# A two-layer graph kernel: where the normalised rows of layer 0 are made and how they are turned

## The reference

```python
# layer 0, 4 heads of 64
h = relu(layernorm(x));  q, k, v = h @ Wq, h @ Wk, h @ Wv
attn = softmax(where(adj, q k^T / 8, -max));  x = x + (attn @ v) @ Wo + bo
# layer 1, 8 heads of 64
h = relu(layernorm(x));  m = h @ map_w.T + map_b;  n = m / |m| per head
cos_adj = (n n^T * ~adj > 0.1)
q, k = m @ q_w.T + q_b, m @ k_w.T + k_b;  p = softmax(where(adj, -1e10, q k^T / 8)) * keep
A = cos_adj * p;  s = h @ gcn_map_w.T + gcn_map_b
x = x + relu((A @ s) @ gcn_W.T / (A.sum(-1) + 1))
```

## Time and profile before

| | before |
|---|---|
| median of three runs | 3766.14 us (3765.32 to 3766.64) |
| the profiled execution | 3767.53 us, its span 3765.7 us |
| TensorE matmul busy | 3665.0 us, 97% of the span |
| VectorE, ScalarE, GpSimd busy | 72%, 45%, 36% |
| mean granted TensorE clock | 0.994 of full |
| queue of SyncE's DMAs | 380.73 MB, 30.4% of 16 engines |
| chain that ended last | PE 89%, DVE 5%, issue 4%, DMA 1% |

### The profile page before, as it was taken

The page is one execution under the profiler, slowest core; times in us unless marked ns, Lnnn a source line. Parts: engine busy times, 40 slices in busy tenths (PEclk is TensorE's granted clock), DMA queues, the critical chain, the costliest instruction groups (busy, mean ns, idle before and its releaser), DMA issues.

```text
span 3765.7 us, 101867 instructions
## 1 busy us (share of the span) xinstructions
PE 3665.0 (97%) x31020; PEld 3224.1 (86%) x31020; DVE 2723.6 (72%) x9432; ACT 1695.4 (45%) x5075; POOL 1357.2 (36%) x2069
## 2 busy tenths in 40 slices
PE   8999999999999999999999999999999999999997
PEld 5888888888888888888888888888888888888885
DVE  3777777777777777777777777777777777777765
ACT  2444444444444444444444444444444444444443
POOL 2333433433433333334334334334333333343331
PEclk9999999999999999999999999999999999999998
DMA  2223323233233233333232332322332333332323
GB/s 94 91 96 106 99 99 107 94 108 102 96 112 102 96 109 100 102 104 104 97 107 98 100 107 94 109 102 96 112 102 96 108 100 102 103 104 98 107 86 107
DMA packets 250601, 381.35 MB, mean 101 GB/s; under 512 B 41328, under 2 KB 173968, under 8 KB 250576
## 3 DMA queue, kind: packets, MB, share of 16 engines
q1 hardware_dynamic: 250304, 380.73, 30.4%
q0 software_dynamic: 272, 0.30, 0.0%
HBM read 179.61 MB, written 167.77 MB: 92 GB/s over the span
## 4 chain that ended last, share of the span: by engine, by line
PE 89%; DVE 5%; issue 4%; DMA 1%; DVEq 1%; POOL 0%; ACT 0%; SPq 0%; POOLq 0%; ACTq 0%
PE bank L949 35%; PE bank L957 19%; PE bank L973 14%; PE bank L981 8%; PE bank L942 7%; PE bank L1090 3%; DVE h L675 1%; DVE x_mid L824 1%; PE bank L1024 1%; PE bank L1102 1%; DVE rel L794 1%; PE bank L898 1%; PE bank L1096 1%; DVE mv L669 0%; DVE rec L785 0%
## 5 line engine op out<-in xcount | busy, mean ns | idle before, releaser
L605 ACT ACTIVATE att<-att,nmax 128x256 f32<-128x256 f32 x1024 | 508.1, 501 | 83.5 <-DVE nmax L760 83.5
L771 DVE SCALAR_TENSOR_TENSOR att<-bank,att 128x256 f32<-128x256 f32 x1024 | 404.9, 421 | 33.0 <-ACT att L605 18.3
L949 PE MATMUL bank<-gT,w_k 128*128 128x256 f32 x3072 | 417.2, 285 | 0.5 <-DVE k L841 0.5
L949 PE MATMUL bank<-gT,w_q 128*128 128x256 f32 x3072 | 414.6, 284 | 2.7 <-DVE w_k L698 1.4
L949 PEld LDWEIGHTS bank<-gT,w_map 128*128 128x128 f32 x3072 | 370.7, 188 | 34.3 <-issue 25.8
L949 PE MATMUL bank<-gT,w_map 128*128 128x256 f32 x3072 | 396.9, 285 | 1.1 <-DVE gT L801 1.1
L949 PE MATMUL bank<-hT,w_qkv 128*128 128x256 f32 x3072 | 392.6, 284 | 4.4 <-DVE hT L801 4.4
L949 PEld LDWEIGHTS bank<-gT,w_k 128*128 128x128 f32 x3072 | 386.7, 189 | 8.2 <-DVE k L841 0.7
L957 PE MATMUL bank<-w_v,gT 128*128 128x512 f32 x1536 | 385.2, 399 | 0.0
L949 PEld LDWEIGHTS bank<-hT,w_qkv 128*128 128x128 f32 x3072 | 373.2, 189 | 13.6 <-DVE w_o L689 4.8
L949 PEld LDWEIGHTS bank<-gT,w_q 128*128 128x128 f32 x3072 | 380.3, 189 | 3.7 <-DVE w_k L698 2.2
(11 more groups left out here) (136 smaller groups left out, 7042.9 us busy)
## 6 DMA issues: line engine op xcount, KB each, us to landing
scratch<-att SPq DMA_DIRECT2D x256, 512.0 KB, 2.6
uT<-scratch SPq DMA_DIRECT2D x1024, 128.0 KB, 3.0
x_in<-x SPq DMA_DIRECT2D x64, 512.0 KB, 3.7
x_res<-x_mid SPq DMA_DIRECT2D x64, 512.0 KB, 2.9
out<-x_res SPq DMA_DIRECT2D x64, 512.0 KB, 2.8
adj<-adj SPq DMA_DIRECT2D x64, 64.0 KB, 1.9
att<-gcn_map SPq DMA_DIRECT2D x1, 1024.0 KB, 10.9
att<-map_rows SPq DMA_DIRECT2D x1, 1024.0 KB, 6.4
```

Source lines behind the costliest of these rows:

```text
L605: s_.activation(e_sl, e_sl, ACT.Exp, bias=nmax1[:, p, c, e:e + 1], scale=-1.0, accum_out=esum1[:, p, c, e:e + 1]).then_inc(exp1_done, 1)
L771: v_.scalar_tensor_tensor(e_sl, in_blocks(gram_bank[e][:, c * N:c * N + N]), COS_THRESHOLD, e_sl, ALU.is_gt, ALU.mult, accum_out=usum1[:, ...
L949: last = t_.matmul(dst, w(ws, k)[:, t * 128:t * 128 + 128], rhs[:, rs, k, :], start=(k == 0 and i == 0), stop=(k == KT - 1 and i == 2))
```

## The change

The rows of layer 0 are no longer normalised by VectorE and turned by TensorE, except for the first graph. `norm0` moves to ScalarE, which computes relu(x * rstd - mean * rstd) straight into `h`, laid out in 32-column blocks. GpSimd makes the new operand `shift0` = -mean * rstd by two small operations behind `rstd0`. Two new VectorE steps, `hflip0` and `hflip1`, transpose `h` in 32x32 blocks in place; two new SyncE steps, `hsend` and `hfetch`, write `h` to DRAM (512 KB) and read it back in four DMAs, so that the blocks land in their places. `ht0a` and `ht0b` keep a place on ScalarE and VectorE only: they split the turned rows, now in SBUF, into high and low parts. The five tables are written anew around this.

```diff
     TENSOR = [
-        ("score", 0), "ht0a", "ht0b", ("k", 2), "qk0", "qk1", ("q", 2), ("cos", 0), "s0", "s1", ("score", 1), "qk2", "qk3",
+        ("score", 0), ("k", 2), ("q", 2), "qk0", "qk1", ("score", 1), ("cos", 0), "s0", "s1", "qk2", "qk3", ("vv", 0), "pt0",
...
     POOL = [
-        ("unit", 0), "mask0", ("unit", 1), "sum0", "mid", "sum1", "sum2", "sum3", "rstd1", ("back", 0), "m0", ("back", 1),
+        ("unit", 0), "mask0", "sum0", ("unit", 1), "mid", "sum1", "sum2", "sum3", "rstd1", ("back", 0), ("back", 1), "m0",
...
     SYNC = [
-        ("spill", 0), "x", ("shift", 0), ("spill", 1), ("shift", 1), ("spill", 2), ("shift", 2), ("spill", 3), ("shift", 3),
-        "adj", ("out", 0), "move"
+        ("spill", 0), ("shift", 0), ("spill", 1), ("shift", 1), "x", ("spill", 2), ("shift", 2), ("spill", 3), "hsend",
+        ("shift", 3), "hfetch", "adj", ("out", 0), "move"
...
+                    elif kind == "hsend":
+
+                        sp.wait_ge(h_flipped, C * n + C)
...
+                        sp.dma_start(scratch_h[:, :, :], h_flips[:, :, :, :, :].rearrange("p b c k f -> p b (c k f)")).then_inc(h_sent, 16)
+                    elif kind == "hfetch":
+
+                        sp.wait_ge(h_sent, 16 * n + 16)
+                        sp.sem_inc(passed_sync, 1)
+                        for cols in range(4):
+                            sp.dma_start(h_turned[32 * cols:32 * cols + 32, :, :, :, :].rearrange("p r c k f -> p r (c k f)"),
+                                         scratch_h[:, cols, :].rearrange("(r p) x -> p r x", p=32)).then_inc(h_in, 16)
...
+            def shift_of(n):
+
+                pool.wait_ge(var_done, 4 * n + 2)
...
+                g.tensor_tensor(shift0[:, :], mv[:, :, 0], rstd[:, :], ALU.mult).then_inc(shift_done, 1)
...
+                g.tensor_scalar(shift0[:, :], shift0[:, :], -1.0, 0.0, ALU.mult, ALU.add).then_inc(shift_done, 1)
...
+                    elif kind[:3] == "ht0":
+                        c = "ab".index(kind[3])
+                        part = hT[:, 0, :, c * 128:c * 128 + 128]
...
+                            act.wait_ge(h_in, 64 * a + 64)
+                            act.wait_ge(product_full, in_psum(a, LAST_OF_HT))
+                            s_.activation(part.rearrange("p k (r f) -> p k r f", f=32), h_turned[:, :, c, :, :], ACT.Copy).then_inc(hT_high, 1)
+                    elif kind == "norm0":
...
+                        for c in range(C):
+                            s_.activation(h_flips[:, :, c, :, :], x_in[:, c, :].rearrange("p (k b f) -> p b k f", b=4, f=32), ACT.Relu,
+                                          bias=shift0[:, c:c + 1], scale=rstd[:, c:c + 1]).then_inc(h0_ready, 1)
...
+                        dve.wait_ge(hT_high, C * n + c + 1)
+                        low, high = [hT[:, i, :, c * 128:c * 128 + 128] for i in (1, 0)]
...
+                            v_.tensor_tensor(low.rearrange("p k (r f) -> p r k f", f=32), h_turned[:, :, c, :, :],
+                                             high.bitcast(F32).rearrange("p k (r f) -> p r k f", f=32), ALU.subtract).then_inc(hT_done, 1)
...
+                    elif kind in ("hflip0", "hflip1"):
...
+                        v_.transpose(blocks, blocks).then_inc(h_flipped, 1)
...
-                        for chunks in (range(2), range(2, 4)):
-                            pe.wait_ge(product_done, out_of_psum(n, "ht0a" if chunks[0] == 0 else "ht0b"))
-                            last = project(full[:, 0:N], lambda s2, k: w_qkv[:, s2, w, k, :], t, hT, chunks)
+                        pe.wait_ge(hT_done, C * n + C)
+                        last = project(full[:, 0:N], lambda s2, k: w_qkv[:, s2, w, k, :], t, hT)
```

More of the change, by code:

```diff
@@ L22, with gnn_two_layers @@
 FLT_MAX = float(np.finfo(np.float32).max)
[L25 removed]
+def gnn_two_layers(nc, x, adj, wq, wk, wv, wo, bo, map_t, map_rows, map_b, q_t, q_b, k_t, k_b, gcn_map, gcn_map_b, gcn_t, out, scratch_h, scratch):
     G, N, D = x.shape
@@ L51, in gnn_two_layers @@
     TENSOR = [
[5 rows of a table removed]
[4 rows of a table added]
+        ("back", 3)
     ]
     SCALAR = [
[4 rows of a table removed]
[4 rows of a table added]
     ]
     VECTOR = [
[L65 to L71, removed]
[3 rows of a table added]
+        ("score_b", 2), "v0", "av", ("back", 0), ("cos_a", 2), ("cos_b", 2), "wo0", "wo1", ("flip_a", 2), ("flip_b", 2),
+        "norm1", ("k", 3), ("q", 3), ("factor", 1), "ht1a", "ht1b", ("score_a", 3), ("back", 1), "stats0", ("cos_a", 3),
+        ("score_b", 3), ("flip_a", 3), ("cos_b", 3), ("factor", 2), ("flip_b", 3), ("factor", 3), "hflip0", "hflip1", "ss",
+        "q0", ("back", 2), "q1", "k0", "rt", "k1", "bc0", "bc1", ("back", 3)
     ]
     POOL = [
-        ("unit", 0), "mask0", ("unit", 1), "sum0", "mid", "sum1", "sum2", "sum3", "rstd1", ("back", 0), "m0", ("back", 1),
-        "m1", "m2", "m3", "rstd0", "pow", ("back", 2), "mask1", ("back", 3)
+        ("unit", 0), "mask0", "sum0", ("unit", 1), "mid", "sum1", "sum2", "sum3", "rstd1", ("back", 0), ("back", 1), "m0",
+        "rstd0", "m1", "m2", "m3", "mask1", "pow", ("back", 2), ("back", 3)
     ]
@@ L83, in gnn_two_layers @@
     OWN = [s for s in PRODUCTS if isinstance(s, str)]
+    LAST_OF_HT = max(("qk0", "qk1", "qk2", "qk3", "v0"), key=OWN.index)
     LATER = [s for s in PRODUCTS if isinstance(s, tuple)]
@@ L240, in gnn_two_layers @@
         h_ready = count("h_ready")
+        h0_ready = count("h0_ready")
+        shift_done = count("shift_done")
+        h_flipped = count("h_flipped")
+        h_sent = count("h_sent")
+        h_in = count("h_in")
+        hT_full = count("hT_full")
+        hT_high = count("hT_high")
+        hT_done = count("hT_done")
         mask0_ready = count("mask0_ready")
@@ L283, in steps @@
             return [s for s in order if (isinstance(s, tuple) and a is not None)
-                    or (isinstance(s, str) and n is not None and (more or s not in ("x", "adj", "stats0", "rstd0", "norm0")))]
+                    or (isinstance(s, str) and n is not None and (more or s not in ("x", "adj", "stats0", "rstd0", "norm0", "hflip0", "hflip1", "hsend", "hfetch")))]
         def in_blocks(ap):
@@ L557, in split_high @@
                 s_.activation(flat(PIECES[k][1][0]), slots[SLOT[k]], ACT.Copy).then_inc(stage_hi, 1)
+            act.wait_ge(shift_done, 2)
+            for c in range(C):
+                s_.activation(h[:, c, :], x_in[:, c, :], ACT.Relu, bias=shift0[:, c:c + 1], scale=rstd[:, c:c + 1]).then_inc(h0_ready, 1)
             for k in range(4):
@@ L610, in body @@
                         s_.activation(oT1[:, :], v_bank[0][:, 0:N], ACT.Copy).then_inc(oT1_ready, 1)
-                    elif kind[:2] == "ht":
+                    elif kind[:3] == "ht0":
+                        c = "ab".index(kind[3])
+                        part = hT[:, 0, :, c * 128:c * 128 + 128]
+                        if a is None:
+                            act.wait_ge(hT_full, C)
+                            s_.activation(part, bank[2 + c][:, :].rearrange("p (k n) -> p k n", n=128), ACT.Copy).then_inc(hT_high, 1)
+                        else:
+                            act.wait_ge(h_in, 64 * a + 64)
+                            act.wait_ge(product_full, in_psum(a, LAST_OF_HT))
+                            s_.activation(part.rearrange("p k (r f) -> p r k f", f=32), h_turned[:, :, c, :, :], ACT.Copy).then_inc(hT_high, 1)
+                    elif kind == "norm0":
+                        act.wait_ge(shift_done, 2 * n + 4)
+                        act.wait_ge(product_full, in_psum(n, "ht1b"))
+                        for c in range(C):
+                            s_.activation(h_flips[:, :, c, :, :], x_in[:, c, :].rearrange("p (k b f) -> p b k f", b=4, f=32), ACT.Relu,
+                                          bias=shift0[:, c:c + 1], scale=rstd[:, c:c + 1]).then_inc(h0_ready, 1)
+                    elif kind[:3] == "ht1":
                         t = 2 * "ab".index(kind[3])
                         act.wait_ge(product_full, in_psum(n, kind))
-                        if kind[2] == "1" and a is not None:
+                        if a is not None:
                             act.wait_ge(later_full, len(LATER) * (a + 1))
-                        dst = hT if kind[2] == "0" else gT
-                        s_.activation(flat(dst[:, 0, t:t + 2, :]), bank[bank_of[kind]][:, :], ACT.Relu).then_inc(high_done, 1)
+                        s_.activation(flat(gT[:, 0, t:t + 2, :]), bank[bank_of[kind]][:, :], ACT.Relu).then_inc(high_done, 1)
                     elif kind[:2] == "qk":
@@ L797, in body @@
                                                 ALU.max, ALU.mult).then_inc(rel_done, 1)
-                    elif kind[:2] == "ht":
+                    elif kind[:3] == "ht0":
+                        c = "ab".index(kind[3])
+                        dve.wait_ge(hT_high, C * n + c + 1)
+                        low, high = [hT[:, i, :, c * 128:c * 128 + 128] for i in (1, 0)]
```

(24 more changed lines are left out.)

24 lines of the change are left out of this document (17 added, 7 removed), and 18 rows, old and new, of tables (SCALAR, TENSOR, VECTOR).

## The result

The changed kernel takes 3854.63 us (median of four runs, 3848.56 to 3854.99) against 3766.24: 1.0231 times as long, 95% interval 1.0214 to 1.0249. Eight transposes a graph are gone and the kernel is 88 us slower. The forecast was 3890.

The account below looks back on a forecast made before the run. TensorE's stream plus its stalls was taken to bound the kernel. Terms -0.85 - 0.05 + 0.55 + 0.15 + 0.55 + 1.65 gave +2.0 us a round, times 63 = +126: forecast 3890 us, range 3740 to 3905.

Parts of the forecast that it names:

- likeliest case: Full wait at `factor`, where VectorE's small operations wait for GpSimd's: 3865 to 3905 us, chance 0.42.
- `wo` to layer 1's transposes: Stall ahead of layer 1's transposes stays; `norm1` starts at 1856.09 against 1856.17, shut out by GpSimd's `x_res` addition: -0.05 a round.
- `av` to `wo`: New TensorE stall ahead of `wo`, covered now only by `back` and `cos`: +0.55 a round, bounds 0.3 and 0.6.
- `rt` to `bc`: TensorE waits 1.41 for VectorE's second copy of `rt`, cover 1.15 to 1.3: +0.15 a round, bounds 0 and 0.25.
- `qk0`: At the round's start `ht0a` and `ht0b` contend with GpSimd's `x_res` and `unit`: +0.55 a round, bounds 0 and 1.35.
- `pt0`: TensorE waits for `qk2`'s bank until 8.1 after S, the start of the s0/s1 products: +1.65 a round, lower bound 0.
- C + 1.38: `den` is due 1.38 after `s0`, `s1`, `flip_a0`, `cos_b0` end on VectorE, 0.11 behind GpSimd's `unit`.
- The DRAM trip: Write and reads of `h` take some 7.5 us, back 1.7 us before ScalarE asks: costed at nothing.
- A: Rival: no lock at the new places, `norm1` as computed: -0.2 a round, 3753 us, chance 0.16.
- B: Rival: no locks, and `norm1` not shut out or `wo` waits less: -0.5 to -1.0 a round, 3705 to 3735, chance 0.16.
- C: Rival: locks only in part, `fac` waits but not `den`, or `ht0b` alone: +0.3 to +0.9, 3785 to 3820, chance 0.22.
- D: Rival: `h` comes back late, stalling `qk0`; a trip of 11 us costs +1.8 a round, 3880 us, chance 0.04.

Follow-up runs that it names:

- experiment 6: Kernel with both moves (first factor ahead of `v0`, `back` 0's addition ahead of `rstd1`), eight 128x128 identity transposes put back ahead of `k2`: 3776.97 us, 1.003.
- experiment 1: Changed kernel with VectorE's first factor moved from ahead of `qk2`'s eviction to directly ahead of `v0`: 3762.52 us, 0.999.
- experiment 2: Kernel before the change, with its first factor moved ahead of the eviction of `qk2`: 3869.71 us, 1.0278.
- experiment 4: Changed kernel with the second unit step back ahead of `sum0` on GpSimd: 3855.58 us, 1.0241.
- experiment 3: Changed kernel with the addition of `back` 0 moved ahead of `rstd1` on GpSimd: 3830.62 us, 1.0176.
- experiment 7: Kernel with both moves (first factor, `back` 0's addition), the 512 KB write of `h` to DRAM done twice ahead of the four reads: 3830.32 us, 1.0176.
- Experiment 5: Changed kernel with first factor ahead of `v0` on VectorE and addition of `back` 0 ahead of `rstd1` on GpSimd: 3737.58 us, 0.9926.

## Why the prediction was right, and where its sizes were off

Direction, mechanism and the place of the largest term were as forecast; the sum was +2.0 a round and 1.35 came. 3854.63 is within the range of 3740 to 3905, which is wide enough to hold a faster kernel too, and below the 3865 to 3905 given for the likeliest case. By its steps, each measured between starts in the round shown:

| step | forecast | measured | from |
|---|---|---|---|
| eight transposes | -0.85 | -0.85 | score to `k2` follow at once; 0.85 again in experiment 6 |
| `wo` to layer 1's transposes | -0.05 | -0.26 | 1895.60 to 1903.33 = 7.73; before 1849.30 to 1857.29 = 7.99 |
| `av` to `wo` | +0.55 | +0.43 | 1892.26 to 1895.60 = 3.34; before `av`, `back`, `cos` 1.78 + 0.22 + 0.91 |
| `rt` to `bc` | +0.15 | +0.26 | 1862.13 to 1863.54 = 1.41; before 1.01 + 0.14 = 1.15 of cover |
| `bc` to score 0 | none | +0.45 | 0.78 + 0.45; before 0.47 + 0.31 |
| `qk0` | +0.55 | +0.1 | `q2` 1.60 to its successor, 1.50 before |
| `pt0` | +1.65 | +1.4 | 4.20 against 2.81 |

These make 1.5; the other 0.2 less is spread over the stream: the remaining score and cos steps take 0.3 less together, two projections that now stand side by side 0.1 less, the `qk` steps 0.2 more and layer 1's transposes 0.1 more.

- **`factor` and `pt0`.** Followed almost to the instruction: `den` requested 1.38 after the reciprocal (forecast C + 1.38), done with the unit step, `fac` with the first addition and not with the second. `pt0` began at S + 7.95 (forecast S + 8.1), its place was S + 6.56 (forecast 6.46). Experiments 1, 2 and 4 show the cause: the wait goes with the factor, comes with it into the other kernel, and doesn't care which GpSimd operation is there.
- **`norm1`.** The lock was there (experiment 3: 24 us), as forecast; but VectorE's statistics came 0.08 sooner behind `wo` (`rstd` 5.44 after its start instead of 5.52), and the first `norm1` operation (1901.79 + 0.96 = 1902.75) ended 0.28 behind the addition (1901.73 + 0.74 = 1902.47) where the forecast's start 0.15 ahead of that end makes it 0.39. So the path was 0.2 shorter than taken. The forecast's own numbers (1856.09 against 1856.17) give -0.08, not -0.05.
- **`ht0a`, `ht0b`.** The mutual shutting out happened (2.67 for the pair), and in the order forecast: low part, unit step, low part. The second ends at 1868.76, 5.22 after `bc` starts; the forecast's times give 1823.38 - 1818.27 = 5.11. That `qk0` lost only 0.1 is because score 0 itself started 0.45 later behind `bc`, by the next term: the same time was lost, but one step earlier. Experiment 6 puts what `hT` costs TensorE there at 0.28, spread over three steps.
- **`rt` to score 0, what was missed.** The 1.41 from `rt` to `bc` came exactly; its cover was 1.15, the low end of what was taken. Behind it the prediction missed a bank: in the new order `bc1` takes the bank of `k1`, whose eviction stands behind `rt` on VectorE (it ends at 1863.92, `bc0` started 1863.54), and the two `bc` steps take 0.78 instead of 0.47. Another 0.14 lies between `back` 3 and score 0 and stays open; ScalarE's copy for `back` 3 ends at 1863.96, before `bc1` is through, and is not its cause. That `bc1` waits for this bank is read from the trace and the program; no run took it away.
- **The DRAM trip** cost nothing on the path, as said, but its cover was 0.7 (an estimate: landing at 1016.75 + 1.3 + 3.7 = 1021.75 in the kernel of experiment 1, used at 1022.46), not 1.7: the write lands in 3.0 us, not 2.6, and the reads in 3.7, not 3.0. In experiment 7 the reads go out later and land in 2.9, so it isn't their size; which traffic slows them no run shows. From the page of the changed kernel:

```profile
scratch_h<-h SPq DMA_DIRECT2D x63, 512.0 KB, 3.0
h<-scratch_h SPq DMA_DIRECT2D x252, 128.0 KB, 3.7
```

- **Rivals.** A and B (no locks) would have needed `den` and `fac` at 0.16. Experiment 5, 3738, comes near B's 3705 to 3735, but only with both waits removed by hand. C is refuted by `den`, D by experiment 7, where the reads had to go out 3.8 us later for TensorE to wait 1.5. D's price of 3880 for a trip of 11 us is 1.8 a round on the kernel before; with A's -0.2 it would be 3867.
- **The misses.** They are mostly on one side: 0.2 at `norm1`, 0.1 at `wo`, 0.25 at `pt0` and 0.2 in the rest of the stream were taken too long, and only the two terms around `rt` and `qk0`, together 0.81 against 0.70, a little too short.

What stays open: the 104 us of experiment 2 against 82 to 94 expected (its `pt0` step takes 4.24 and the one behind it 0.15 more, together 1.58 a round, 100 us; why the second step grows isn't known), and the share of the 0.45 that belongs to the bank.

## What to carry to other kernels

Taking work off the busiest engine pays its place in the stream (here 39 of a nominal 54 us), and a new order can lose twice that at one place. Where VectorE operations with two inputs in SBUF, or tensor_scalar from SBUF to SBUF, stand near long GpSimd operations, look at their longest duration, not their mean: a 128x4 operation at 1.2 us is a wait that VectorE's idle time doesn't show. Before a restructuring is judged, the same defect should be looked for in the kernel before: there one step moved (in three tables) gave 27 us, as much as the whole restructuring after repair, 28.

## What was not expected of the hardware

A short VectorE operation that waits gets in between two GpSimd operations that follow each other without a gap (`den` between `nrm` and `x_mid`, `fac` between the two additions). A long one holds GpSimd up in turn: the unit step 1.74 for 1.30, the mask 0.94 for 0.62. And GpSimd's `rn` operation of 2.9 us on 128x16 numbers does not stretch the VectorE operation beside it. In the kernel before, GpSimd and VectorE at 1813:

```profile
1813.04 2.90 POOL L547 TENSOR_TENSOR rn<-ssq,minus_half 128x16 f32<-128x16 f32 x1 [1.23 <-DVE ssq L846]
```

```profile
1813.28 0.16 DVE L788 TENSOR_TENSOR fac<-rec,keep 128x4 f32<-128x4 f32 x1
```

`fac` runs inside `rn` and keeps its 0.16, where the one beside the x_res addition took 0.71. The first `norm0` operation (1815.29, 0.54) lies inside `rn` too and isn't stretched. So what decides is not that GpSimd is busy, but with which operation. It matters on VectorE's side too: in the changed kernel all 256 `rec` operations, which read one tile, take 178 to 182 ns, and all 512 flips of `att` 669 to 717, whatever GpSimd does beside them.
